# Two graph and expert layers on one core: in the second experts' stage VectorE writes the upper part of the activated rows

## The reference, cut to what matters

```python
def _L1_ffn_ref(x, gate_w, w1, b1, w2, b2):
    gate_logits = x_flat @ gate_w.T
    topk_vals, topk_idx = jax.lax.top_k(gate_logits, 2)
    comb = ...                                   # softmax of the two, zero elsewhere
    for e in range(8):
        h = jax.nn.gelu(x_flat @ w1[e].T + b1[e], approximate=False)   # 256 -> 1024
        y = h @ w2[e].T + b2[e]                                        # 1024 -> 256
        out = out + comb[:, e:e + 1] * y
```

## Time and profile before

| | us |
|---|---|
| median of 3 runs | 1857.75 (1856.11 to 1861.74) |
| the profiled execution's own time | 1856.73 |
| its span | 1855.0 |
| PE busy | 1562.9 (84%) |
| DVE busy | 1175.9 (63%) |
| ACT busy | 596.3 (32%) |
| POOL busy | 750.9 (40%) |

### The profile page before, as it was taken

One profiled execution on the slowest core, in us unless ns is written; L12 is line 12 of the kernel. 1 busy time (PEld: TensorE's weight loads), 2 busy tenths in 40 slices (PEclk: granted clock), 3 DMA queues, 4 the chain that ended last, 5 costly groups with the idle time before them and its releaser, 6 DMA issues. The chain is left out here.

```text
span 1855.0 us, 35707 instructions
## 1 busy us (share of the span) xinstructions
PE 1562.9 (84%) x9584; PEld 1302.8 (70%) x9584; DVE 1175.9 (63%) x3915; ACT 596.3 (32%) x1264; POOL 750.9 (40%) x1362
## 2 busy tenths in 40 slices
PE   5899999999999917999999059999339998889894
PEld 4888888888888706878878036555228888888894
DVE  5467777777677685666565427666776656666652
ACT  2333333333233302223323123222114544444452
POOL 0123223222322104777776534434324554555452
PEclk9899999999999957999999579999659999999998
DMA  7224433334443171233333234655421222221223
GB/s 115 96 107 143 153 140 127 127 134 145 147 147 127 54 278 38 46 51 51 51 47 50 80 119 144 217 193 199 175 84 29 35 39 31 34 33 32 34 40 91
DMA packets 85362, 184.70 MB, mean 100 GB/s; under 512 B 19789, under 2 KB 62539, under 8 KB 81291
## 3 DMA queue, kind: packets, MB, share of 16 engines
q1 hardware_dynamic: 57386, 128.02, 21.1%
q0 software_dynamic: 22656, 31.07, 10.7%
q10 hardware_dynamic: 5280, 25.17, 3.4%
HBM read 132.66 MB, written 54.99 MB: 101 GB/s over the span
## 5 line engine op out<-in xcount | busy, mean ns | idle before, releaser
L1113 PE MATMUL bank<-ffn_w_in_parts,ffn_x_t 128*128 128x512 f32 x1416 | 363.0, 405 | 1.3 <-DVE ffn_w_in_parts L1243 1.3
L1137 PE MATMUL bank<-ffn_w_out_parts,ffn_hidden_t 128*128 128x256 f32 x2124 | 291.6, 293 | 35.9 <-DVE ffn_hidden_t L1233 35.8
L1137 PEld LDWEIGHTS bank<-ffn_w_out_parts,ffn_hidden_t 128*128 128x128 f32 x2124 | 270.0, 196 | 42.7 <-DVE ffn_w_out_parts L1243 23.6
L1113 PEld LDWEIGHTS bank<-ffn_w_in_parts,ffn_x_t 128*128 128x128 f32 x1416 | 260.4, 191 | 56.0 <-DVE ffn_w_in_parts L1243 4.5
L659 PE MATMUL bank<-support,attn_probs_t 128*128 128x512 f32 x650 | 247.9, 414 | 5.2 <-DVE attn_probs_t L533 4.8
L624 PE MATMUL bank<-h_t,attn_h_tile 128*128 128x512 f32 (+1 forms) x1092 | 248.9, 383 | 3.9 <-POOL attn_h_tile L493 3.9
L624 PEld LDWEIGHTS bank<-h_t,attn_h_tile 128*128 128x128 f32 x1092 | 196.9, 189 | 46.2 <-issue 4.1
L1077 POOL DMA_INDIRECT x<-ffn_y,ffn_dst x118 | 194.4, 1648 | 54.2 <-issue 54.2
L521 ACT CAST attn_probs_t<-bank 128x512 fp32r<-128x512 f32 (+1 forms) x182 | 98.6, 557 | 358.9 <-PE bank L633 358.9
L1179 ACT ACTIVATE ffn_silu_or_gelu<-bank,w_b_in 128x128 f32<-128x128 f32 x472 | 134.2, 367 | 218.6 <-PE bank L1124 218.6
L661 PE MATMUL bank<-support,attn_probs_t 128*128 128x256 f32 x676 | 185.5, 281 | 0.0
(11 more groups left out here) (247 smaller groups left out, 2505.3 us busy)
## 6 DMA issues: line engine op xcount, KB each, us to landing
adj_tile<-in_adj SPq DMA_DIRECT2D x25, 1663.5 KB, 7.2
mask<-attn_mask ACTq DMA_DIRECT2D x26, 832.0 KB, 3.4
nbr_mask<-mask SPq DMA_DIRECT2D x26, 832.0 KB, 5.1
w_w_in<-in_w SPq DMA_DIRECT2D x16, 512.0 KB, 10.3
w_w_in<-in_w_t SPq DMA_DIRECT2D x16, 512.0 KB, 4.1
w_w_out<-in_w SPq DMA_DIRECT2D x1, 4096.0 KB, 20.2
x<-attn_x_out SPq DMA_DIRECT2D x26, 128.0 KB, 1.7
xn<-attn_x_normed SPq DMA_DIRECT2D x26, 128.0 KB, 2.3
```

What stands on the lines that cost most here:

```text
L1113: ins = pe.matmul(bank[2 + 2 * slot + b][:, :], XT[:, slot, xp, k, :], WIP[:, wp, k, b * CH:(b + 1) * CH], start=n == 0 and k == 0, stop=n ...
L1137: ins = pe.matmul(bank[7][:, 0:D], HTT[:, hp, k, :], WOP[:, wp, k, :], start=n == 0 and k == 0, stop=n == 2 and k == KH - 1)
```

## The change

For the ungated stage, ACT's own wait and its copy into the upper part are gone: ACT goes on to the next half's GELUs at once. DVE waits for `gelu_ready` of the half, and for `second_done` (the tile before has been multiplied), makes the copy and raises the same signal `ht_hi`, for which it then waits itself, as before, ahead of its subtraction. The gated stage's ACT copy keeps its source, the bank.

```diff
@@ hidden_out, on ACT
                             ins.then_inc(gelu_ready, 1)
-                            act.wait_ge(gelu_ready, t * HB + j + 1)
+                            continue
                         if not known(t) or t >= 1:
                             act.wait_ge(second_done, t)
                         act.copy(HTT[:, 0, 4 * j:4 * j + 4, :],
-                                 (src[:, :] if gated else GATE[:, j, :]).rearrange("p (k n) -> p k n", n=P)).then_inc(ht_hi, 1)
+                                 src[:, :].rearrange("p (k n) -> p k n", n=P)).then_inc(ht_hi, 1)
@@ hidden_rest, on DVE
                         src = h_bank[slot][:, :] if gated else GATE[:, j, :]
+                        if not gated:
+                            dve.wait_ge(gelu_ready, t * HB + j + 1)
+                            if not known(t) or t >= 1:
+                                dve.wait_ge(second_done, t)
+                            dve.tensor_copy(HTT[:, 0, 4 * j:4 * j + 4, :], src.rearrange("p (k n) -> p k n", n=P)).then_inc(ht_hi, 1)
                         dve.wait_ge(ht_hi, t * HB + j + 1)
```

## The result

The changed kernel took 1865.35 us (median of 22 runs), the one before 1856.99 us (22 runs): ratio 1.0044, 95% interval 1.0033 to 1.0055, 8.2 us (6.1 to 10.2). The time lies in the stated range (1855 to 1868), but the likeliest case, no change that can be told, did not come; slower had been given 0.23. The span of the profiled execution grew from 1855.0 to 1860.8 us.

A forecast was written before the change was run, and what follows sets the result against it. PE, idle for DVE (23.4 and 14.2 us) at 7 changes of expert and the stage's ends, bounds the kernel; -3.8 + 6.0 + 0.8 - 0.4 - 0.2 = +2.4 us gives 1859.1, with the median's 1.0, 1860 us; range 1855 to 1868.

The forecast's parts named there:

- rival 1: Half 0 late in every even tile, from a copy of about 0.51 us on: 1870 us, chance 0.12.
- rival 2: Granted clock at changes of expert: another drop each, 1871 us (slower, 0.08), or clock kept up, 1851 us (faster, 0.07).
- step T-2, T even: First stall at 5 changes of expert, ACT late: half 1 ready 0.44 us sooner, start limited by DVE's sequencer.
- step T-2, T odd: First stall at 2 changes of expert, ACT late: half 1 ready 0.81 us sooner at each.
- step T-1: Second stall, before T-1's second layer, DVE late: copy and hand-over add 0.46 us at 6 of 7 changes.
- step T: Third stall, before T's second layer, DVE late after splitting weights: 0.46 us more at all 7 changes.
- even tiles inside an expert: Away from changes: half 0's room shrinks from 0.27 to 0.09 us; 0.05 us lost in each of 16, 0.8 us.
- first and last tile: Ends of the stage, where PE waited for the halves: 0.4 us saved in the first, 0.2 in the last.
- 5 x 0.44: Saving in the first stall at the 5 changes with T even: 0.44 us each, from 1.78 to 1.34 us.
- at the one at 1416.79 it is covered: Step T-1 at this change of expert costs nothing, since no stall of the second layer followed before.
- Rival 3: DVE's copy waits for POOL's whole indirect DMA in even tiles: +30, 1888 us, chance 0.03.
- A copy over 0.51 us: Sign that the prediction is wrong: DVE's copy, expected at 0.42 us, taking longer than this.

The follow-up runs named there:

- e1: Kernel before, with DVE copying only half 1 into the upper part and ACT still copying half 0: 1856.21 us, ratio 0.9996.
- e9: Changed kernel, with DVE's load of the expert's number moved between the two halves of `hidden_rest`: 1855.26 us, ratio 0.9995 to the kernel before.
- e10: Kernel before (ACT makes both copies), with DVE's load of the expert's number moved between the two halves of `hidden_rest`: 1847.74 us, ratio 0.9960.
- e2: Kernel before, with DVE copying only half 0 into the upper part and ACT still copying half 1: 1863.55 us, ratio 1.0032.
- e7: e1, with ACT instead of DVE making the second half of the copy of the first layer's result: 1848.71 us, ratio 0.9955.
- e8: Kernel before, with ACT instead of DVE making the second half of the copy of the first layer's result: 1848.96 us, ratio 0.9959.
- e11: Kernel before (ACT makes both upper-part copies) with the moves of e10 and e8 together: 1845.06 us, ratio 0.9933.
- e12: Changed kernel (DVE makes both upper-part copies) with the moves of e10 and e8 together: 1849.48 us, ratio 0.9959 to the kernel before.
- e13: e1 (DVE copies half 1 only) with the moves of e10 and e8 together: 1844.15 us, ratio 0.9948 to the kernel before.

## Why the prediction was right and wrong

The mechanism of the stalls was the one predicted, at the places named, but the sum was under a third of what came. Of the 5.8 us that it lacks 2.6 are in PE's stalls, and some 3 lie outside them, in no term of the sum. That the time fell into the range is in part luck: the range was wide because it took in half of rival 1 and of the slower rival 2. By the prediction's own terms, from PE's idle times before and after (the ends also count 0.5 us of shorter matmuls, and 0.16 us more of waiting before the stage's first transposes, where no copy was moved, is left out; so the sum is 5.0 and not 5.6):

| term | predicted | measured |
|---|---|---|
| step T-2, T even (5) | -2.2 | -0.5 (1.77 to 1.66 us) |
| step T-2, T odd (2) | -1.6 | -2.0 |
| step T-1 (7) | +2.8 | +4.7 |
| step T (7) | +3.2 | +3.6 |
| even tiles inside an expert (16) | +0.8 | 0 |
| first and last tile | -0.6 | -0.8 |
| sum | +2.4 | +5.0 |
| all of the time | +2.4 | +8.2 |

The price of a late step was right in kind: 0.43 for the copy, 0.04 for the hand-over, and some 0.06 that DVE's start lies later behind the result (0.60 us after it and not 0.53), where the code has one more wait: 0.51 to 0.54 for the 0.46 taken.

**The first step that failed** is "5 x 0.44" in step T-2. The start of the copy I had at 1.15 us after the result's end; it was 1.23. And the sum stopped at the subtraction's end, as if what follows would move with it. What follows is a branch and another register load on DVE's sequencer, and it took longer at the earlier time. The load of the expert's number ahead of the weight split, before and after (DVE's sequencer by line; the duration in ns three times, and the start):

```profile
L1039 DVEq TENSOR_LOAD <-route_expert x1: 338/338/338, 1467.5 to 1467.5; - x1
```

```profile
L1039 DVEq TENSOR_LOAD <-route_expert x1: 449/449/449, 1464.9 to 1464.9; - x1
```

From the second subtraction's end to the weights' cast it was 0.32 us before and 0.57 after. So 0.36 of the 0.44 us reached the subtraction and 0.11 reached PE. In e1 the same load took 0.44 us at this place, and PE came no sooner either. In e9, with the other load out of the way, DVE's copy started 0.45 us earlier, this load took 0.31 us, and the first stall fell to 1.25. Why it took longer in the changed kernel is not settled.

**The second** is "at the one at 1416.79 it is covered". Before, the first layer's 12 matmuls behind the stall of 2.03 us took 4.58 us, in a stretch granted 0.76 of the full clock, and that hid DVE's lateness. After, the stall there is 0.91, the 12 take 3.03, as in other tiles, and the second stall shows in full, 1.46 us. The two groups, before and then after, and before's stretch (us, busy PE PEld DVE ACT POOL, granted clock, DMA share, GB/s):

```profile
1417.63 4.58 PE L1113 MATMUL bank<-ffn_w_in_parts,ffn_x_t 128*128 128x512 f32 x12
...
1414.82 3.03 PE L1113 MATMUL bank<-ffn_w_in_parts,ffn_x_t 128*128 128x512 f32 x12
...
1416.00:1423.00 7.00, 6.21 (x29) 5.22 (x30) 5.76 (x15) 3.79 (x11) 2.31 (x5) 0.76 0.04 2
```

From the start of the transposes to that of the second layer it was 5.40 us before and 5.55 after. So 1.3 of the 1.46 us is not a loss but the other side of the missing slow stretch: a cover that is a slow stretch of PE is no cover. A slow stretch does not follow every such stall: in e10, behind one of 2.04 us at the same place, the 12 matmuls took 3.03 us.

**The third** is the time outside the stalls. I gave the clock as a rival, with a drop more at every change; what came is milder, and it goes for most kernels here. For each, PE's idle time for DVE in the stage (L1137 and L1124, one profile), the change of time by the ratio, and the granted clock averaged over the span and over all runs, its own and that of the kernel before in the runs beside it (for the changed kernel's none are on record):

| kernel | PE idle, us | against before | time, us | clock | before's clock |
|---|---|---|---|---|---|
| before | 37.6 | | | | 0.9302 to 0.9309 |
| changed | 43.2 | +5.6 | +8.2 | 0.9289 | |
| e1 | 38.0 | +0.4 | -0.7 | 0.9313 | 0.9305 |
| e2 | 39.9 | +2.3 | +5.9 | 0.9298 | 0.9305 |
| e7 | 34.1 | -3.5 | -8.4 | 0.9327 | 0.9309 |
| e8 | 34.4 | -3.2 | -7.6 | 0.9331 | 0.9309 |
| e9 | 36.7 | -0.9 | -0.9 | 0.9308 | 0.9309 |
| e10 | 34.7 | -2.9 | -7.4 | 0.9325 | 0.9302 |
| e11 | 30.1 | -7.5 | -12.4 | 0.9330 | 0.9302 |
| e12 | 31.0 | -6.6 | -7.6 | 0.9300 | 0.9302 |
| e13 | 29.2 | -8.4 | -9.7 | 0.9324 | 0.9302 |

The clock's difference times the span is a time: a microsecond at half the clock takes 0.5/1860 off the mean, and costs 0.5 us where PE is at work. For the changed kernel that is 0.0013 to 0.0020 x 1860 = 2.4 to 3.7 us, and its time rose by 2.6 us more than the stalls; for e10 0.0023 x 1860 = 4.3 us against 4.5, for e8 4.1 against 4.4, for e11 5.2 against 4.9, for e7 3.3 against 4.9. e2 (1.3 against 3.6), e12 (0.4 of the other sign against 1.0 gained) and e13 (4.1 against 1.3) fit less well, within what their intervals allow. So the rest of the loss, about a third, goes with a lower granted clock. The one profiled pair does not show it: in the stage the second layer's matmuls took 2.3 us more (192.7 to 195.0), the first layer's 2.3 us less (180.6 to 178.3), and the profiled execution of the changed kernel, at 1862.64 us, lies below its median.

In the profiles the slow clock is seen as groups of 24 matmuls that take 4.2 to 4.6 us in place of 3.11 behind a stall of 2.4 to 3.1 us; the changed kernel has them at 7 of 7 changes, one of 5.46 us, before it was 6 of 7, and e10 shows 3 of 7. The third stall's length does not decide it: e8 has before's third stalls (2.47 to 2.56 us) and shows 3 of 7, and in e2 the 24 behind a stall of 3.09 us took 3.11. e8 differs from the kernel before in the first stall, 1.16 for 1.78 us. That more idle time in all makes the drops more frequent fits most of the rows; but each profile is one execution, and no run varied a stall and nothing else, so this stays argued.

**The signs that were named.** PE's idle time before L1137 came to 31.3 us for the 29 forecast, and before L1124 to 11.9 for 11. The groups of 24 that are slow at a change went from 6 to 7, and a change in their number had been named as a sign that the prediction is wrong. A copy over 0.51 us was another: 27 of the 118 copies took 0.54 to 0.59, but all of them are half 1's; half 0's, which PE's second and third stall wait for, took 0.48 at most.

**What held:** rival 1 did not come (no gap of PE in any even tile inside an expert, and half 0's copy at 0.43 us, as the earlier trace rows had it), but by 0.02 us and not by 0.09. Rival 3 did not come either: the cast at 1614.82, inside a scatter of 1613.92 to 1615.66, took 0.56 us for 0.43 and ended before it. The Trainium skill's rule of a lock held for the whole instruction (SBUF — State Buffer, "Who interferes with whom") would have had it wait to 1615.66; the trace shows 0.13 us on one side and 0.14 on the other (the scatter took 1.74 for 1.60). Those are the two neighbouring rows:

```profile
1613.92 1.74 POOL L1077 DMA_INDIRECT x<-ffn_y,ffn_dst  x1 [0.51 <-issue]
...
1614.82 0.56 DVE L1236 CAST ffn_hidden_t<-ffn_silu_or_gelu 128x512 fp32r<-128x512 f32 x1
```

## What to carry to other kernels

Ask of each place where the bottleneck engine stalls who is late there: moving work from an idle engine to the late one loses at every such place, though the engines' averages (here ACT 32%, DVE 63%) promise room, and only where the giver is late does it win. The saving has to be followed to the next instruction of the chain, through branches and register loads, and not only to the end of the operation that became earlier. Where PE's clock drops behind stalls, a stall is worth more than its length: here 1.5 times for the changed kernel, about 2.5 for e2, e7, e8 and e10, and hardly more than its length for e12 and e13.

## What the runs showed of the hardware that I had not expected

- A register load of 0.30 us on DVE's sequencer, which no table of busy time counts, was worth 0.4% (7.4 us, 2.9 of it in PE's stalls) once it stood under a subtraction and not ahead of one.
- A wait that a view puts down to ACT can be the sequencer's: 1.23 us "for ACT" in even tiles, where ACT had been done for 0.5 us; without the splits' branches the same wait was 0.78.
- A cast on DVE and an indirect DMA of POOL slow each other by a little, and only at certain places. All 27 copies of 0.54 to 0.59 us began 0.83 to 1.00 us into a scatter, and those scatters took 1.66 to 1.87 us for 1.60; copies that began 0.38 or 1.45 us into one took 0.43 and 0.42, and the scatter 1.60.
- The time spreads from run to run, 22 runs of the changed kernel from 1857.23 to 1872.0 us and of the one before from 1851.76 to 1861.74, and in part it goes with the clock: over the changed kernel's runs the correlation of time and granted clock is -0.6.
